# Layer 2's rows go to fixed expert regions of a bucket, right behind the last gather

## The chip, the core and the metric

One core of a Trainium2 chip runs the kernel. The metric is the device time of one execution in microseconds (us), so smaller is better. The engines are PE (TensorE; PEld is its weight load), DVE (VectorE), ACT (ScalarE), POOL (GpSimd) and SP (SyncE, which here only issues DMAs). PE's clock has two levels here, 1.2 and 2.4 GHz; the profile gives the granted clock as a share of full speed (0.5 or 1.0, or a mean of both).

## What is computed

Node features `x` (6250 x 256) pass a two-layer relational graph network over 100000 edges with 8 relations, a linear-attention mixer, and a feed-forward block in which each node uses one of 32 experts:

```python
xn = _layernorm(x)
x = x + gnn(edge_index, edge_type_8, xn) + mix(xn)          # gnn: 2 layers
x = x + ffn(_layernorm(x))

# gnn, each layer l
W = einsum('rb,bio->rio', coeffs[l], bases[l]); h = einsum('ni,rio->rno', x, W)
msg = h[edge_type, src] * deg_inv[dst][:, None]
x_new = segment_sum(msg, dst) + x @ self_loops[l]           # relu after layer 1

# ffn: E = 32 experts, hidden 64
idx = argmax(xf @ router_w.T + router_b)
h = relu(xf . W1[idx] + b1[idx]);  out = relu(h . W2[idx] + b2[idx])
```

## The kernel before

The nodes are cut into NB = 49 blocks of 128. `startup` (L128) norms x, builds the relation weights and writes table 0 (one row per node and relation) to DRAM. `gnn_first` (L541) and `gnn_second` (L812) are the two layers; `experts` (L1063) is the feed-forward block. Each of these is a block of five engine programs with a barrier of all engines at its end.

**A layer.** POOL gathers message rows: each indirect DMA (L487) brings 128 table rows, four DMAs are a group, and the ring holds RG = 16 groups. POOL waits for PE before it uses a group again (L483 to L485). PE sums a block's groups with one-hot matrices that DVE makes (L514, L530), in a loop with run-time bounds. SP counts landed groups. A block's matmul sum opens with a zero matmul (L523) and closes with one (L537). In `gnn_second` each step n also runs stages of other blocks: query, attention, output, norm, router, choice of the expert, and with a lag of 6 blocks the row's rank among the rows of its expert (PE L990 and L991, DVE L905 and L919, in `r.rank`). So the last sum is at step 48 and the last rank at step 54; steps 49 to 54 have no sum.

During `gnn_first`, SP writes zero rows with an out-of-range node number over the whole `bucket` in DRAM (L594, 16 DMAs of 650 KB): rows that no node fills are skipped in the end.

**The experts.** After the barrier, SP loads the weights w1 and w2 (L1107, L1108; 2064 and 2080 KB). They lie where the ring lay. PE counts the rows of each expert (L1158), and DVE turns counts into the tile each expert starts at (L1216 to L1222), each node's row in the bucket (`posi`, L1225 to L1229, blocks 0 to 7 first), and the expert of each tile (`tei`, L1230 to L1234, which ends with `tiles_ok`). POOL scatters the 49 blocks of rows, 260 numbers each, to the bucket (L1125). Experts lie behind each other there, each padded to whole tiles; there are MAXT = 80 tiles at most and all 80 are always processed. When all scatters have landed SP loads the tiles, four to a DMA, into a ring of XS = 40 (L1115). PE runs WARM = 116 matmuls whose result nobody uses (L1164) once `tiles_ok`, the weights and `nearly` (the fifth-last scatter's issue) are there. Then come the 40 pairs of tiles: DVE norms (L1201), PE transposes (L1140), ACT copies (L1254) and copies the pair's weights (L1252), PE multiplies (L1147), ACT adds the bias (L1261), PE multiplies (L1153), DVE adds to the row (L1208), and POOL scatters each tile to `out` (L1131). A tile's ring place is free when that scatter has landed.

## Time and profile before

| | us |
|---|---|
| median of 3 runs | 3634.85 |
| the three runs | 3616.99, 3634.85, 3636.49 |
| the profiled execution | 3627.62 |
| its span, first to last instruction | 3625.9 |

| stretch of the profiled execution, us from the span's start | what runs |
|---|---|
| to 406 | startup |
| 406 to 2010 | gnn_first |
| 2010 to 3366 | gnn_second; the last gather is issued at 3297.7 |
| 3366 to 3461 | experts: tables, scatters, weights, 116 matmuls of no use |
| 3461 to 3619 | experts: 40 pairs of tiles |

Over the span PE is busy 66%, PEld 48%, POOL 45%, DVE 25%, ACT 18%. These are averages over stages with different limits. A table row "start, duration" in the timeline merges neighbouring instructions of one kind (xN), and what stands in brackets is the idle time ahead of it and what ended it.

### The profile page before, as it was taken

What the parts mean: (1) busy time and instruction counts of PE and PEld (TensorE: products, weight loads), DVE (VectorE), ACT (ScalarE), POOL (GpSimd) and SP (SyncE); (2) the same over time, 40 slices, a digit from 0 to 9 for tenths busy, and PEclk for the clock granted to TensorE, in tenths of its full rate; (3) what the DMA queues carried; (4) which work ended last, traced back from release to release, by engine and by line L of the source; (5) the groups of instructions that cost most, each with busy time, mean ns of one, the idle gap of its engine ahead of it and who ended that gap; (6) DMA issues with size and microseconds to landing.
All of it is one profiled execution on the core that took longest, in us unless ns stands there. A gap on an engine that the chain in (4) does not pass through costs nothing. (4 is left out here: it accounts for less than half of the span.)

```text
span 3625.9 us, 37652 instructions
## 1 busy us (share of the span) xinstructions
PE 2399.8 (66%) x9592; PEld 1739.3 (48%) x9592; DVE 915.7 (25%) x2885; ACT 652.3 (18%) x1423; POOL 1649.7 (45%) x1712
## 2 busy tenths in 40 slices
PE   6999346666666666666578356676666667657287
PEld 3777234444444444444456244454444545445065
DVE  2210112222222222222123023233332323324233
ACT  4555101110111011111111101111212112110033
POOL 0000654445444444445451646556565555652535
PEclk9999668878887888778789678777777777878577
DMA  8655533333333333333332323333333333321341
GB/s 220 231 218 195 156 95 112 106 107 103 112 102 104 103 110 109 106 103 113 100 121 75 121 77 92 89 88 91 87 90 88 89 92 89 90 84 46 128 128 53
DMA packets 155518, 401.32 MB, mean 111 GB/s; under 512 B 35102, under 2 KB 86657, under 8 KB 140348
## 3 DMA queue, kind: packets, MB, share of 16 engines
q0 software_dynamic: 81648, 219.65, 20.8%
q10 hardware_dynamic: 36156, 126.22, 9.0%
q1 hardware_dynamic: 37585, 53.92, 5.5%
q8 instruction: 58, 0.95, 0.1%
q14 instruction: 71, 0.58, 0.1%
HBM read 262.69 MB, written 141.04 MB: 111 GB/s over the span
## 5 line engine op out<-in xcount | busy, mean ns | idle before, releaser
L487 POOL DMA_INDIRECT gnn_ring<-table,g_idx x1564 | 1513.1, 967 | 1627.0 <-PE gnn_pagg L530 857.3
L530 PE MATMUL gnn_pagg<-gnn_ring,gnn_oh 128*128 x3904 | 1124.5, 432 | 427.7 <-issue 378.6
L530 PEld LDWEIGHTS gnn_pagg<-gnn_ring,gnn_oh 128*128 128x128 f32 x3904 | 775.7, 212 | 775.3 <-issue 662.9
L514 DVE TENSOR_TENSOR gnn_oh<-gnn_col,g_dst 128x256 f32<-128x256 f32 x976 | 408.3, 426 | 1803.6 <-DVEq L49 1609.9
L715 PE MATMUL gnn_pm<-gnn_whigh,gnn_high 128*128 128x512 f32 x392 | 202.4, 516 | 480.1 <-ACT gnn_rows L769 473.1
L769 ACT COPY gnn_rows<-gnn_pm 128x512 f32<-128x512 f32 x196 | 110.9, 587 | 1320.9 <-DMA pre_bs<-in_L_gnn_bases 1082.7
L715 PEld LDWEIGHTS gnn_pm<-gnn_whigh,gnn_high 128*128 128x128 f32 x392 | 94.4, 241 | 520.0 <-ACT gnn_rows L769 493.4
L1026 ACT ACTIVATE gnn_qe<-gnn_pq,gnn_bq 128x128 f32<-128x128 f32 x98 | 36.0, 368 | 1061.1 <-remote 1045.6
L715 PE MATMUL gnn_pm<-gnn_wlow,gnn_high 128*128 128x512 f32 x392 | 188.0, 480 | 0.0
L715 PE MATMUL gnn_pm<-gnn_whigh,gnn_low 128*128 128x512 f32 x392 | 186.7, 476 | 0.0
L366 PE MATMUL pre_psum<-pre_whigh,pre_high 128*128 128x512 f32 x392 | 157.5, 402 | 10.6 <-DVE pre_low L294 8.1
L366 PE MATMUL pre_psum<-pre_whigh,pre_low 128*128 128x512 f32 x392 | 153.7, 392 | 0.0
L366 PE MATMUL pre_psum<-pre_wlow,pre_high 128*128 128x512 f32 x392 | 153.3, 391 | 0.0
L417 ACT COPY pre_rows<-pre_psum 128x512 f32<-128x512 f32 x196 | 114.6, 589 | 118.1 <-PE pre_psum L366 108.4
L1131 POOL DMA_INDIRECT out<-g_xT x80 | 80.0, 1000 | 99.9 <-DVE g_xT L1208 78.8
L715 PEld LDWEIGHTS gnn_pm<-gnn_whigh,gnn_low 128*128 128x128 f32 x392 | 94.9, 242 | 25.0
L715 PEld LDWEIGHTS gnn_pm<-gnn_wlow,gnn_high 128*128 128x128 f32 x392 | 96.4, 246 | 18.7
L696 PE MATMUL gnn_pk<-gnn_wkv,g_xT 128*128 128x512 f32 x196 | 98.0, 623 | 0.0
L1125 POOL DMA_INDIRECT bucket<-rt_x,exp_posi x49 | 51.2, 1045 | 89.4 <-DVE exp_posi L1229 74.7
L366 PEld LDWEIGHTS pre_psum<-pre_whigh,pre_high 128*128 128x128 f32 x392 | 74.1, 189 | 25.1 <-DVE pre_low L294 8.5
L366 PEld LDWEIGHTS pre_psum<-pre_whigh,pre_low 128*128 128x128 f32 x392 | 73.9, 188 | 15.9
L366 PEld LDWEIGHTS pre_psum<-pre_wlow,pre_high 128*128 128x128 f32 x392 | 74.2, 189 | 14.2
(172 smaller groups left out, 2210.0 us busy)
## 6 DMA issues: line engine op xcount, KB each, us to landing
table<-pre_rows ACTq DMA_DIRECT2D x49, 1024.0 KB
table<-gnn_rows ACTq DMA_DIRECT2D x48, 1024.0 KB
gnn_ring<-table,g_idx POOLq DMA_INDIRECT x1564
pre_bs<-in_L_gnn_bases SPq DMA_DIRECT2D x64, 240.0 KB
bucket<-gnn_zrow SPq DMA_DIRECT2D x16, 650.0 KB
g_xT<-bucket SPq DMA_DIRECT2D x20, 520.0 KB, 6.3
x1T<-gnn_x1T ACTq DMA_DIRECT2D x49, 128.0 KB
gnn_x1T<-x1T ACTq DMA_DIRECT2D x49, 128.0 KB, 2.1
```

The lines of the kernel that those rows point to most:

```text
L366: mm = nc.tensor.matmul(psum[:, n, 0:hi - lo], x[i][:, h, :], w[j][:, h, lo:hi], start=(h == i + j == 0), stop=(h == H2 - 1 and i == 1))
L417: nc.scalar.copy(rows[:, b % 2, lo:hi], psum[:, n, 0:hi - lo]).then_inc(chunk_free, 1)
L487: eng.indirect_dma_start(self.ring[:, q % RG, t, 0:D], None, self.g.table[self.l][:, :], bass.IndirectOffsetOnAxis(ap=self.g.idx[:, at:at ...
L514: self.nc.vector.tensor_tensor(self.oh[:, h, :, :], self.col[:, :].unsqueeze(1).to_broadcast([P, n, P]), self.g.dst[:, ds(q * TPG + h * n, ...
L530: mm = nc.tensor.matmul(pagg[:, k, 0:self.width], self.oh[:, h, i, :], self.ring[:, ds(q & (RG - 1), 1), t, 0:self.width].rearrange("p o n ...
L696: mm = nc.tensor.matmul(pk[:, :], g.xT[:, h, b * P:(b + 1) * P], wkv[:, h, :], start=(h == 0), stop=(h == H2 - 1))
L715: mm = nc.tensor.matmul(pm[:, n % W, 0:CW], x[i][:, h, :], w[j][:, h, n * CW:(n + 1) * CW], start=(h == i + j == 0), stop=(h == H2 - 1 and ...
L769: ins = nc.scalar.copy(rows[:, k, n * CW:(n + 1) * CW], pm[:, n % W, 0:CW])
L1026: nc.scalar.activation(qe[:, k, h, :], pq[:, h * P:(h + 1) * P], ACT.Exp, bias=bq[:, h:h + 1])
L1125: eng.indirect_dma_start(g.bucket[:, :], bass.IndirectOffsetOnAxis(ap=posi[:, b:b + 1], axis=0), r.x2[:, b, :], None).then_inc(scattered, 16)
L1131: eng.indirect_dma_start(out[:, :], bass.IndirectOffsetOnAxis(ap=xb[:, t % XS, D:D + 1].bitcast(I32), axis=0), xb[:, t % XS, 0:D], None, b ...
```

## The change

- The bucket has 6400 rows for each expert (CAP) and 128 spare ones. A row's place is expert x 6400 + rank, which needs no counts. PE adds expert x 6400 to the rank with one more matmul in each of 49 steps (new L1009), and DVE turns the sum into an integer with one more instruction in each (new L943). `g.placed` counts blocks whose places are known.
- POOL's 49 scatters stand behind its last gather in `gnn_second`. The first waits for 38 placed blocks, each one after block 37 for its own.
- `gnn_second` and `experts` are one block of programs: no barrier and no clearing of semaphores between them. The experts' work on SP, PE, ACT and DVE waits for `g.left` = 2 instead (DVE and ACT done with `gnn_second`).
- A tile's first row comes from a table (`rowi`). An expert's last tile is its last 128 rows, so it can share rows with the tile ahead of it; `skip` marks these, and DVE puts the mark into the node number with one more instruction per tile (new L1223). Only the first 128 rows of each expert and the spare ones are written with zeros ahead: 8 DMAs of 4 x 128 rows and one of 128, instead of 16 of 5 x 128.
- DVE's work for the positions goes; instead of one multiply-sized and one reduce instruction over 2560 elements there are three and three.
- SP loads one tile per DMA, from an address in a register, into a ring of XS = 20; it waits for `tiles_ok` as well as for the scatters.

```diff
-XS, XG = 40, 4
+XS, XG = 20, 4
+CAP = 6400
...
-        self.bucket = dram("bucket", (MAXT * P, ROW), F32)
+        self.bucket = dram("bucket", (E * CAP + P, ROW), F32)
...
             def zeros(q):
 
-                if q % 12 == 6 and q // 12 < ZERO:
-                    c = q // 12
-                    eng.dma_start(g.bucket[c * ZT * P:(c + 1) * ZT * P, :].rearrange("(t p) d -> p t d", p=P),
-                                  zrow[:, :].unsqueeze(1).to_broadcast([P, ZT, ROW])).then_inc(zeroed, 16)
+                c, at = divmod(q, 20)
+                if at == 6 and c < FILLS:
+                    first = g.bucket[0:E * CAP, :].rearrange("(e c) d -> c e d", c=CAP)[0:P, c * EF:(c + 1) * EF, :]
+                    eng.dma_start(first, zrow[:, :].unsqueeze(1).to_broadcast([P, EF, ROW])).then_inc(zeroed, 16)
+                elif at == 6 and c == FILLS:
+                    eng.dma_start(g.bucket[E * CAP:, :], zrow[:, :]).then_inc(zeroed, 16)
...
+            for b in range(NB):
+                if b == 0 or b > SURE:
+                    eng.wait_ge(g.placed, max(b, SURE) + 1)
+                eng.indirect_dma_start(g.bucket[:, :], bass.IndirectOffsetOnAxis(ap=r.posi[:, b:b + 1], axis=0),
+                                       r.x2[:, b, :], None).then_inc(g.scattered, 16)
+                if b == NB - 5:
+                    eng.sem_inc(g.nearly, 1)
...
+                if ranked:
+                    V.tensor_copy(r.posi[:, ds(n - 6, 1)], r.rank[:, ds(n - 6, 1)]).then_inc(g.placed, 1)
...
+            eng.wait_ge(g.placed, NB)
+            eng.sem_inc(g.left, 1)
...
-                    nc.tensor.matmul(po[:, k, D:D + E], g.one[:, :], r.acc[:, j, :], start=True, stop=False)
+                    nc.tensor.matmul(po[:, k, D:D + E], g.one[0:2, :], ecap[:, :], start=True, stop=False)
+                    nc.tensor.matmul(po[:, k, D:D + E], g.one[:, :], r.acc[:, j, :], start=False, stop=False)
...
+            nc.scalar.copy(idle[:, 1:2], bq[:, 0:1]).then_inc(g.left, 1)
...
-        x_in = [s.sem(f"x_in{k}") for k in range(XS // XG)]
+        x_in = [s.sem(f"x_in{k}") for k in range(XS)]
-        block = ctx.enter_context(nc.Block())
...
+            eng.wait_ge(g.left, 2)
             eng.dma_start(w1[:, :, :], a["ffn_first"]).then_inc(w_in, 16)
             eng.dma_start(w2[:, :, :], a["ffn_second"]).then_inc(w_in, 16)
+            eng.wait_ge(tiles_ok, 1)
             eng.wait_ge(scattered, 16 * NB)
-            for c in range(MAXT // XG):
-                lo = c * XG % XS
-                for u in range(lo, lo + XG):
-                    if c * XG >= XS:
-                        eng.wait_ge(landed[u], 16 * (c * XG // XS))
-                eng.dma_start(xb[:, lo:lo + XG, :], g.bucket[c * XG * P:(c + 1) * XG * P, :].rearrange("(t p) d -> p t d", p=P)
-                              ).then_inc(x_in[c % (XS // XG)], 16)
+            for t in range(MAXT):
+                if t % XG == 0:
+                    at = values(rowi[0:1, t:t + XG], engines=[eng.engine], min_val=0, max_val=E * CAP,
+                                skip_runtime_bounds_check_because="a tile lies in its expert's rows or the spare ones")[1]
+                if t >= XS:
+                    eng.wait_ge(landed[t % XS], 16 * (t // XS))
+                eng.dma_start(xb[:, t % XS, :], g.bucket[ds(at[t % XG], P), :]).then_inc(x_in[t % XS], 16)
...
-            for b in range(NB):
-                if b == 0 or b == EARLY:
-                    eng.wait_ge(pos_ok, 1 if b == 0 else 2)
-                eng.indirect_dma_start(g.bucket[:, :], bass.IndirectOffsetOnAxis(ap=posi[:, b:b + 1], axis=0),
-                                       r.x2[:, b, :], None).then_inc(scattered, 16)
-                if b == NB - 5:
-                    eng.sem_inc(nearly, 1)
...
-            eng.wait_ge(nearly, 1)
+            eng.wait_ge(g.nearly, 1)
...
-                if t % XG == 0:
-                    eng.wait_ge(x_in[t % XS // XG], 16 * (t // XS + 1))
+                eng.wait_ge(x_in[t % XS], 16 * (t // XS + 1))
...
                 x = xb[:, t % XS, :]
+                node = x[:, D:D + 1].bitcast(I32)
+                V.tensor_tensor(node, node, skip[:, t:t + 1], ALU.max)
                 V.tensor_scalar(xf[:, t % 8, :], x[:, 0:D], x[:, D + 1:D + 2], x[:, D + 2:D + 3],
                                 ALU.subtract, ALU.mult).then_inc(xf_ok, 1)
...
+            V.memset(last[:, E:], float(E * CAP))
+            seq(V.tensor_scalar(over[:, :], cnt[:, 0, :], -float(2 * P - 1), 0.0, ALU.add, ALU.max))
+            seq(V.scalar_tensor_tensor(out=last[:, 0:E], in0=g.iota[:, 0:E], scalar=float(CAP), in1=over[:, :],
+                                       op0=ALU.mult, op1=ALU.add))
+            V.tensor_tensor(step[:, 1, :], last[:, 1:], last[:, 0:E], ALU.subtract)
...
-            seq(V.tensor_scalar(cnt[:, 3, :], cnt[:, 2, :], float(P), None, ALU.mult))
...
-            for lo, hi in ((0, EARLY), (EARLY, NB)):
-                seq(V.tensor_tensor(by_block(part, lo, hi), by_block(r.oh, lo, hi),
-                                    cnt[:, 3, :].unsqueeze(1).to_broadcast([P, hi - lo, E]), ALU.mult))
-                seq(V.tensor_reduce(pos[:, 0, lo:hi], by_block(part, lo, hi), AX.X, ALU.add))
-                seq(V.tensor_tensor(pos[:, 1, lo:hi], pos[:, 0, lo:hi], r.rank[:, lo:hi], ALU.add))
-                V.tensor_copy(posi[:, lo:hi], pos[:, 1, lo:hi]).then_inc(pos_ok, 1)
             seq(V.tensor_tensor(cnt[:, 0, :], cnt[:, 1, :], cnt[:, 2, :], ALU.add))
-            seq(V.tensor_tensor(tl[:, :, :], cnt[0:1, 0, :].unsqueeze(1).to_broadcast([1, MAXT, E]),
-                                g.iota[0:1, 0:MAXT].unsqueeze(2).to_broadcast([1, MAXT, E]), ALU.is_le))
-            seq(V.tensor_reduce(te[:, :], tl[:, :, :], AX.X, ALU.add))
-            V.tensor_scalar(tei[:, :], te[:, :], float(E - 1), None, ALU.min).then_inc(tiles_ok, 1)
+            V.tensor_scalar(step[:, 0, :], cnt[:, 1, :], -float(P), float(CAP), ALU.mult, ALU.add)
+            seq(V.tensor_tensor(tl[:, 0, :, :], cnt[:, 0, :].unsqueeze(1).to_broadcast([P, MAXT, E]),
+                                g.iota[:, 0:MAXT].unsqueeze(2).to_broadcast([P, MAXT, E]), ALU.is_le))
+            for k in range(2):
+                ins = V.tensor_tensor(tl[:, 1 + k, :, :], tl[:, 0, :, :], step[:, k, :].unsqueeze(1).to_broadcast([P, MAXT, E]),
+                                      ALU.mult)
+            seq(ins)
+            for k in range(3):
+                ins = V.tensor_reduce(te[:, k, :], tl[:, k, :, :], AX.X, ALU.add)
+            seq(ins)
+            V.tensor_scalar(tei[:, :], te[0:1, 0, :], float(E - 1), None, ALU.min)
+            seq(V.scalar_tensor_tensor(out=te[:, 3, :], in0=g.iota[:, 0:MAXT], scalar=float(P), in1=te[:, 1, :],
+                                       op0=ALU.mult, op1=ALU.add))
+            seq(V.scalar_tensor_tensor(out=te[:, 1, :], in0=te[:, 2, :], scalar=last[:, 0:1], in1=te[:, 3, :],
+                                       op0=ALU.add, op1=ALU.min))
+            V.tensor_copy(rowi[:, :], te[0:1, 1, :]).then_inc(tiles_ok, 1)
+            V.tensor_copy(part[:, :], g.nodei[:, 0:1])
+            seq(V.tensor_tensor(twice[:, :], te[:, 3, :], te[:, 1, :], ALU.subtract))
+            seq(V.tensor_scalar(skip[:, :], twice[:, :], part[:, 0:1], float(SKIP), ALU.is_gt, ALU.mult))
             for t in range(6):
...
-        gnn_second(nc, g, a, r)
-        nc.clear_and_free_semaphores(nc.allocated_since(had))
-        nc.all_engine_barrier()
-        experts(nc, g, a, r, out)
+        with nc.Block() as block:
+            gnn_second(nc, g, a, r, block)
+            experts(nc, g, a, r, out, block)
```

POOL, from its last gathers to the tiles' scatters. Before (`rt_x` holds the rows, `exp_posi` the places; the semaphore names after "waits" are older ones of the same numbers, here the places of blocks 0 to 7 and of the rest):

```order
L487 DMA gnn_ring<-table,g_idx 128x256 [waits gnn1_pairs]
L487 DMA gnn_ring<-table,g_idx 128x256 x5
L819 UNCONDITIONAL_BRANCH
L1287 ISA [waits barrier_Pool_Activation_PE_DVE_SP_gather]
L1120 UNCONDITIONAL_BRANCH [waits barrier_Pool_Activation_PE_DVE_SP_gather]
L1125 DMA bucket<-rt_x,exp_posi 10240x260 [waits pre_x_in1]
L1125 DMA bucket<-rt_x,exp_posi 10240x260 x7
L1125 DMA bucket<-rt_x,exp_posi 10240x260 [waits pre_x_in1]
L1125 DMA bucket<-rt_x,exp_posi 10240x260 x40
L1131 DMA out<-g_xT 6250x256 [waits pre_var_ok] x80
```

The same place in the change:

```order
L489 DMA gnn_ring<-table,g_idx 128x256 [waits gnn1_pairs]
L489 DMA gnn_ring<-table,g_idx 128x256 x5
L886 DMA bucket<-rt_x,rt_posi 204928x260 [waits g_placed]
L886 DMA bucket<-rt_x,rt_posi 204928x260 x37
L886 DMA bucket<-rt_x,rt_posi 204928x260 [waits g_placed] x11
L1148 UNCONDITIONAL_BRANCH
L1152 DMA out<-g_xT 6250x256 [waits exp_y_ok] x80
```

The 49 scatters have moved ahead of the end of `gnn_second`, and the barrier between them and the gathers is gone.

DVE, from the tiles' first numbers (`exp_cnt`) to `tiles_ok`. Before:

```order
L1225 TENSOR_TENSOR exp_part<-rt_oh,exp_cnt 128x256 [waits g_dve_own]
L1227 TENSOR_REDUCE exp_pos<-exp_part 128x8 [waits g_dve_own]
L1228 TENSOR_TENSOR exp_pos<-exp_pos,rt_rank 128x8 [waits g_dve_own]
L1229 CAST exp_posi<-exp_pos 128x8 [waits g_dve_own]
L1225 TENSOR_TENSOR exp_part<-rt_oh,exp_cnt 128x1312
L1227 TENSOR_REDUCE exp_pos<-exp_part 128x41 [waits g_dve_own]
L1228 TENSOR_TENSOR exp_pos<-exp_pos,rt_rank 128x41 [waits g_dve_own]
L1229 CAST exp_posi<-exp_pos 128x41 [waits g_dve_own]
L1230 TENSOR_TENSOR exp_cnt<-exp_cnt 128x32
L1231 TENSOR_TENSOR exp_tl<-exp_cnt,g_iota 1x2560 [waits g_dve_own]
L1233 TENSOR_REDUCE exp_te<-exp_tl 1x80 [waits g_dve_own]
L1234 TENSOR_SCALAR exp_tei<-exp_te 1x80 [waits g_dve_own]
```

In the change (`g_xT` stands for the table of 3 x 2560 that lies in its memory):

```order
L1251 TENSOR_TENSOR exp_cnt<-exp_cnt 128x32 [waits g_dve_own]
L1252 TENSOR_SCALAR exp_step<-exp_cnt 128x32 [waits g_dve_own]
L1253 TENSOR_TENSOR g_xT<-exp_cnt,g_iota 128x2560
L1256 TENSOR_TENSOR g_xT<-g_xT,exp_step 128x2560 [waits g_dve_own]
L1256 TENSOR_TENSOR g_xT<-g_xT,exp_step 128x2560
L1260 TENSOR_REDUCE exp_te<-g_xT 128x80 [waits g_dve_own]
L1260 TENSOR_REDUCE exp_te<-g_xT 128x80 x2
L1262 TENSOR_SCALAR exp_tei<-exp_te 1x80 [waits g_dve_own]
L1263 SCALAR_TENSOR_TENSOR exp_te<-g_iota,exp_te 128x80
L1265 SCALAR_TENSOR_TENSOR exp_te<-exp_te,exp_last 128x80 [waits g_dve_own]
L1267 CAST exp_rowi<-exp_te 1x80 [waits g_dve_own]
```

The eight instructions on positions are gone; two instructions over 2560 elements have become six, and three small ones follow.

## Rows read from the trace of the kernel before

**Rows 1.** The page: PE's busy tenths in 40 equal slices of the span.

```profile
PE   6999346666666666666578356676666667657287
```

**Rows 2.** Timeline, POOL: last gather, first scatter; start, duration, in brackets idle ahead.

```profile
3297.66 0.95 POOL L487 DMA_INDIRECT gnn_ring<-table,g_idx  x1 [0.30 <-issue]
3373.36 2.02 POOL L1125 DMA_INDIRECT bucket<-rt_x,exp_posi  x1 [74.74 <-DVE exp_posi L1229]
```

**Rows 3.** Source view of the scatters' line: ns min/median/max, first and last start.

```profile
L1125 POOL DMA_INDIRECT bucket<-rt_x,exp_posi x49: 970/974/3399, 3373.4 to 3438.2; - x49
```

**Rows 4.** Timeline, DVE: last rank, then the tables.

```profile
3364.61 0.19 DVE L919 TENSOR_REDUCE rt_rank<-gnn_ch 128x1 f32<-128x32 f32 x1
3366.41 0.48 DVE L1212 MEMSET exp_hT<- 1x512 f32 x1 [1.61 <-PEq L1288]
...
3371.57 0.18 DVE L1222 TENSOR_SCALAR exp_cnt<-exp_cnt 128x32 f32<-128x32 f32 x1
...
3372.98 1.52 DVE L1225 TENSOR_TENSOR exp_part<-rt_oh,exp_cnt 128x1312 f32<-128x1312 bf16 x1
...
3376.42 0.23 DVE L1230 TENSOR_TENSOR exp_cnt<-exp_cnt 128x32 f32<-128x32 f32 x1
3376.70 2.81 DVE L1231 TENSOR_TENSOR exp_tl<-exp_cnt,g_iota 1x2560 f32<-1x2560 f32 x1
...
3382.39 0.19 DVE L1234 TENSOR_SCALAR exp_tei<-exp_te 1x80 int32<-1x80 f32 x1
```

**Rows 5.** Timeline, ACT: its first use of the weights.

```profile
3386.83 0.50 ACT L1252 COPY exp_ws<-exp_w 128x129 f32 x2 [24.59 <-DMA exp_w<-in_ffn_second]
```

**Rows 6.** Timeline, PE: the 116 matmuls and the first transposes.

```profile
3418.92 12.60 PE L1164 MATMUL exp_psum<-rt_oh,g_one 128*128 128x512 bf16 x45 [52.46 <-issue]
...
3444.87 16.11 PE L1164 MATMUL exp_psum<-rt_oh,g_one 128*128 128x512 bf16 x66 [0.82 <-issue]
3460.82 1.04 PE L1140 MATMUL exp_psum<-g_ident,exp_xf 128*128 128x128 f32 x8
```

**Rows 7.** Timeline, SP and DVE: the tiles' loads and the first norms.

```profile
3440.78 33.12 SPq L1115 DMA_DIRECT2D g_xT<-bucket  x11
3444.47 2.87 DVE L1201 TENSOR_SCALAR exp_xf<-g_xT 128x256 f32<-128x256 f32 x8 [61.88 <-DMA g_xT<-bucket]
```

**Rows 8.** Timeline, PE: zero matmuls opening blocks 0, three others, 46, 47 and 48.

```profile
2067.85 0.21 PE L523 MATMUL gnn_pagg<-g_zero 128*128 128x2 bf16 x1
...
2582.10 0.17 PE L523 MATMUL gnn_pagg<-g_zero 128*128 128x2 bf16 x1
2614.85 0.16 PE L523 MATMUL gnn_pagg<-g_zero 128*128 128x2 bf16 x1 [2.41 <-issue]
2634.54 0.17 PE L523 MATMUL gnn_pagg<-g_zero 128*128 128x2 bf16 x1
...
3303.23 0.17 PE L523 MATMUL gnn_pagg<-g_zero 128*128 128x2 bf16 x1
3320.03 0.17 PE L523 MATMUL gnn_pagg<-g_zero 128*128 128x2 bf16 x1
3336.65 0.17 PE L523 MATMUL gnn_pagg<-g_zero 128*128 128x2 bf16 x1
```

**Rows 9.** Timeline, DVE in the pairs of tiles: two pauses.

```profile
3475.76 0.76 DVE L1208 SCALAR_TENSOR_TENSOR g_xT<-exp_psum,g_xT 128x256 f32<-128x256 f32 x2 [3.29 <-DMA gnn_ring<-table,g_idx]
...
3500.08 0.76 DVE L1208 SCALAR_TENSOR_TENSOR g_xT<-exp_psum,g_xT 128x256 f32<-128x256 f32 x2 [3.25 <-DMA gnn_ring<-table,g_idx]
```

**Rows 10.** Source views, us to landing: tiles' scatters (L1131), tiles' loads (L1115).

```profile
DMA to landing us min/median/max: 2.5/2.5/2.5
...
DMA to landing us min/median/max: 3.7/6.3/10.3
```

**Rows 11.** Timeline, PE: the transposes of two pairs in a row, at full clock.

```profile
3465.68 0.60 PE L1140 MATMUL exp_psum<-g_ident,exp_xf 128*128 128x128 f32 x4
...
3468.20 0.60 PE L1140 MATMUL exp_psum<-g_ident,exp_xf 128*128 128x128 f32 x4
```

50 lines of the change are left out of this document (31 added, 19 removed).

## The prediction

> **What bounds the kernel now.** The page's 40 slices come first [rows 1]: in the slices of layer 2 PE is 5 to 7 tenths busy and no engine is full. Then comes one slice, the 38th (3354 to 3445 us), with PE at 2 tenths. That slice is the place of the change. The timeline shows what stands in it. POOL issues its last gather at 3297.66 and its first scatter at 3373.36, 74.74 us later [rows 2]; PE meanwhile drains the ring. The last rank is made at 3364.61, the barrier takes 1.61 us of DVE, and the tables follow [rows 4]. The 49 scatters run from 3373.4 to 3438.2 and set the pace: 64.8 us for 48 steps, 1.35 us each [rows 3]. The first tile load is issued at 3440.78 and the first norm starts at 3444.47 [rows 7]. But PE starts its first transpose only at 3460.82, since the 116 matmuls of no use are still running [rows 6]. So the wait that ends last ahead of the pairs is that of PE for its own 116 matmuls, 16.4 us later than the first tile. From the last rank's end (3364.8) to PE's first transpose it is 96.0 us.
>
> **What goes.** The scatters leave this stretch. At POOL's last gather 38 places have to be known for the first scatter. PE opens block 46 at 3303.23 [rows 8], so step 45 is at its end at 3298, and with a lag of 6 blocks about 40 places are known: the first wait is met at once or within a few us. From 3299, at 0.97 + 0.30 us each, block 40 goes out at about 3351 [rows 2, 3]; the last 8 wait for their ranks, the last of which is made at 3364.8. The last scatter lands about 4 us later. The positions' instructions go as well, and so do the barrier and its 1.6 us.
>
> **What bounds the stretch afterwards.** The tables: PE's 116 matmuls and SP's loads both wait for `tiles_ok`. Before, DVE needed 3366.41 to 3382.58 for them, 16.2 us [rows 4]. Of this 3371.57 to 3376.42 goes, 4.85 us. Two instructions over 2560 elements become six; they cost 2.81 us on one partition. I take the same on 128 partitions, because the one over 1312 elements on 128 partitions takes 1.52 us, 1.16 ns per element beside 1.10 here [rows 4]. That adds 4 x 2.81 = 11.2. Some nine small ones at 0.2 add 1.8. So 16.2 - 4.9 + 11.2 + 1.8 = 24.3 us. The weights were there at 3386.83, 20.4 us after DVE's start on the tables and beside scatters [rows 5]; they stay covered by the tables, by 4 us. The scatters are covered by 20 us.
>
> Then come the 116 matmuls, now alone: the first 13 or so at PE's lower clock of 1.2 GHz at 0.43 us, the others at 0.215. The two runs of 45 and 66 show this: 12.6 and 16.1 us, the second with 8 at the lower clock [rows 6]. That is 5.6 + 22.1 = 27.7 us. The tile loads hide behind them: the first norm came 3.7 us after the first load [rows 7], 20 loads of 133 KB are fewer bytes than the 40 tiles before.
>
> Handover from layer 2: 0.5 us. Sum: 0.5 + 24.3 + 27.7 = 52.5 us in place of 96.0. **Gain 43.5 us**, if layer 2 ends when it did.
>
> **What it costs ahead of that.** (a) POOL now sends scatters while PE, DVE and ACT drain the ring. Before, that stretch had no DMAs of POOL, and blocks 46 and 47 took 16.8 and 16.6 us; under gathers 46 blocks took 1235.4 us, 26.9 each [rows 8]. Part of the 26.9 is POOL's own pace (16 gathers at 0.95 + 0.30 us are 20 us [rows 2]), which scatters don't impose. The rest looks like starved engines. The same is seen where PE's 116 matmuls run beside scatters: from 3431.5 to 3444.87 PE starts only 116 - 45 - 66 = 5, where it does one in 0.215 to 0.43 us otherwise [rows 6]. Bounds: nothing, and two blocks (what fits into the 52 us of scatters without a pause) at 26.9 instead of 16.7, 20 us. A small gain from a shift of the steps can't be excluded, but no row shows one. I take 15, nearer to the upper end, since the row of the 116 matmuls is of scatters themselves.
>
> (b) One matmul and one copy more in each of 49 steps. A small DVE instruction lasts 0.2 us [rows 4], and its successor can overlap part of it; PE's lasts no longer. Nothing if they fall into a pause of their engine, 0.2 us per step if they are on the path in full: 0 to 10 us. I take 5, the middle.
>
> (c) In the pairs: DVE has two more small instructions per pair (0.2 us each at most), beside 0.76 for the results and 2 x 0.36 for the norms [rows 7, 9] in a pair of 2.52 us at the full clock [rows 11]. Its slack is 1.0 us, so nothing; at most 0.4 x 40 = 16 us if it had none. SP issues 80 loads instead of 20 and reads four addresses for four of them; eleven issues took 33 us only because they waited for places [rows 7]; it has 1.25 us per tile. Nothing.
>
> (d) The ring of 20. A tile's place goes round: scatter 1.0 us, landing 2.5, SP's turn 0.5, load 3.7 (up to 10.3 with four tiles in one DMA) [rows 3, 10]: 8 us, 14 at worst. Between the result of tile t and the norm of tile t+20 DVE works on seven pairs, 17.6 us at the full clock. Nothing.
>
> (e) Seven fewer fill DMAs in layer 1, 6 MB of writes in some 1500 us: nothing.
>
> **Sum.** 43.5 - 15 - 5 = 23.5 us off 3627.6, the profiled execution's own time: 3604. This execution lies 7.2 us below the median of the three runs and 10.6 above the lowest. I put the forecast a little above, at **3608**, between the profile's sum and the median's (3611).
>
> The Trainium skill ("Runtime: NRT & Kernel Launch", section on instruction fetch mechanics) says that instructions come in blocks of 256 and that crossing from one to the next is mostly hidden. By that rule nothing starves beside POOL's DMAs and term (a) would be zero. The trace speaks against it in the pairs: there DVE stands still for 3.29 and 3.25 us at 3475.76 and 3500.08, 24 us apart [rows 9], about as long as 256 of PE's instructions last.
>
> **Rivals.**
> 1. The drain is not disturbed: (a) is 0 and (b) small. Scatters move as many bytes as gathers, but it was only one slow piece in 65 us of them [rows 3, 6]. Then 43.5 - 2.5 = 41 us: 3587 on the profile, about 3592. Chance 0.22. The rule of the skill above leads here.
> 2. The 116 matmuls meet another slow piece and the drain costs its full 20, the steps 10: 43.5 - 20 - 10 - 12 = 1.5 us gained, 3626 to 3634. For it: the slow piece took 13.4 us once [rows 6]. Against: POOL is silent then. Chance 0.12.
> 3. The ring of 20 starves the pairs: if the round trip were 25 us instead of 8, each of three turns of the ring would wait some 7 to 10 us, 25 us in all: about 3630. Against: the sum in (d). Chance 0.08.
> 4. Slower: the added instructions shift layer 2's pauses. Its blocks come in two kinds, as 32.8 and 19.7 us in a row [rows 8]; each that turns from short to long costs about 13 us. With two more long ones the gain of 23.5 is gone; with four the kernel is about 29 us slower, near 3660. For it: 26.9 is a mean of both kinds, so the mix matters. Against: the change adds 98 PE instructions to a layer with thousands. Chance 0.08.
>
> That the scatters start no earlier (the first wait not met) would show as a POOL pause after 3298; a few us of it cost nothing, since block 48's rank ends the row.
>
> **How the numbers follow.** Forecast (3596 to 3620) 0.50; rivals 0.22, 0.12, 0.08, 0.08. The range takes in rival 1, the forecast, and rivals 2 and 3: 3586 to 3634; below it lies little, above it rival 4. A measurement tells 0.5% (18 us) from no change here. Faster by over 0.5% means under 3616.7: rival 1 and nearly all of the forecast, 0.67. Within 0.5%: the rest of the forecast and rivals 2 and 3, 0.23. Slower: rival 4 and a little of the others, 0.10.
>
> **What would show it.** First scatter within 5 us of the last gather, the last landed before the tables end. Blocks 46 and 47 between 17 and 27 us long: their length decides between the forecast and rival 1. `tiles_ok` 24 to 25 us after the last place; PE's 116 matmuls in 28 us; first transpose 52 to 53 us after layer 2's end. From PE's first transpose to the end about 165 us as before; waits of the norms for their loads would be rival 3. Blocks 1 to 46 of layer 2 at 26.9 us plus 0.1: more is rival 4. The prediction is wrong if DVE's instructions over 2560 elements cost more on 128 partitions, or if something outside this stretch moves.

## The result, and the profile after

The changed kernel takes 3643.09 us (median of 15 runs, 3634.79 to 3650.49), the kernel before, measured beside it, 3629.56 us (15 runs, 3612.07 to 3645.48). The ratio is 1.0048 with a 95% interval of 1.0031 to 1.0065: a little slower, where 3608 us and a gain were forecast. The profiled execution of the changed kernel took 3639.18 us, with a span of 3637.4 us and a mean granted clock of 0.807 (before: 3627.62, 3625.9 and 0.801).

The head of the experts' part came out as forecast. Behind the last rank stand the tables and then PE's 116 matmuls, without a slow piece. The rows are DVE's and PE's timeline of the changed kernel (start, duration, in brackets the idle time before and what ended it), to be read beside [rows 4] and [rows 6]:

```profile
3428.51 0.15 DVE L943 CAST rt_posi<-rt_rank 128x1 int32<-128x1 f32 x1
...
3452.64 0.19 DVE L1267 CAST exp_rowi<-exp_te 1x80 int32<-1x80 f32 x1
```

```profile
3452.89 26.97 PE L1186 MATMUL exp_psum<-rt_oh,g_one 128*128 128x512 bf16 x116 [23.86 <-DVE exp_rowi L1267]
3479.69 1.04 PE L1161 MATMUL exp_psum<-g_ident,exp_xf 128*128 128x128 f32 x8
```

From the last rank's end (3428.7) to the end of `exp_rowi` it is 24.2 us, where 0.5 + 24.3 were forecast; the 116 matmuls take 27.0 (27.7). PE's first transpose starts 51.0 us behind the last rank, in place of 96.0.

What was gained there was lost one stage earlier. The scatters do start right behind the last gather, and 40 of them go out without a pause, as POOL's timeline shows (line 489 gathers, line 886 scatters):

```profile
3309.62 0.95 POOL L489 DMA_INDIRECT gnn_ring<-table,g_idx  x1 [0.30 <-issue]
3310.87 1.00 POOL L886 DMA_INDIRECT bucket<-rt_x,rt_posi  x1 [0.30 <-issue]
...
3360.67 0.97 POOL L886 DMA_INDIRECT bucket<-rt_x,rt_posi  x1 [0.30 <-issue]
3382.19 0.97 POOL L886 DMA_INDIRECT bucket<-rt_x,rt_posi  x1 [20.55 <-DVE rt_posi L943]
```

Meanwhile block 46 of layer 2 stands. PE's timeline has the zero matmuls (line 525) that open blocks 46, 47 and 48, to be read beside the last of [rows 8], and the sums over the ring between them, and ahead of them the matmuls (line 1020) whose result ACT takes next; then come the one row of DVE and the one of ACT that end their idle time:

```profile
3314.14 0.53 PE L1020 MATMUL gnn_pq<-gnn_rw,gnn_turned 128*128 128x32 f32 x4
3315.04 0.17 PE L525 MATMUL gnn_pagg<-g_zero 128*128 128x2 bf16 x1
3316.97 2.18 PE L532 MATMUL gnn_pagg<-gnn_ring,gnn_oh 128*128 x8 [1.76 <-PEq L50]
3368.89 12.80 PE L532 MATMUL gnn_pagg<-gnn_ring,gnn_oh 128*128 x40 [49.74 <-PEq L50]
3384.47 0.17 PE L525 MATMUL gnn_pagg<-g_zero 128*128 128x2 bf16 x1
3386.57 10.54 PE L532 MATMUL gnn_pagg<-gnn_ring,gnn_oh 128*128 x40 [1.93 <-issue]
3399.90 0.17 PE L525 MATMUL gnn_pagg<-g_zero 128*128 128x2 bf16 x1
```

```profile
3368.12 0.76 DVE L516 TENSOR_TENSOR gnn_oh<-gnn_col,g_dst 128x256 f32<-128x256 f32 x2 [51.59 <-DVEq L50]
```

```profile
3365.68 0.18 ACT L1049 COPY gnn_lg<-gnn_pq 128x32 f32<-128x32 f32 x1 [64.70 <-remote]
```

Block 46 takes 3384.47 - 3315.04 = 69.4 us in place of 16.8; block 47 takes 15.4. PE did one turn of its loop over groups and DVE one of its, and then nothing ran but POOL. The three don't stand in the same way. Line 50 belongs to the helper `take`, which waits for a semaphore. PE waits there for DVE's next one-hots: the first is made at 3368.54, and PE goes on at 3368.89. DVE waits for a free place for its one-hots, which PE's 8 matmuls had given it by 3319.15, yet it goes on only at 3368.12. ACT has what it waits for at 3314.67 and goes on 51.0 us later. So what has to be explained is why DVE and ACT stand; PE, here, waits for DVE. The table by stretch (busy time and number of instructions of each engine) says it in one line:

```profile
core 0: us, PE busy (x) PEld busy (x) DVE busy (x) ACT busy (x) POOL busy (x), PEclk, DMA share, GB/s
...
3330.00:3362.00 32.00, 0.00 (x0) 0.00 (x0) 0.00 (x0) 0.00 (x0) 24.26 (x25) 0.50 0.29 104
3368.00:3384.00 16.00, 14.94 (x55) 11.09 (x56) 7.76 (x30) 0.00 (x0) 0.97 (x1) 0.80 0.02 7
```

In 32 us three engines execute no instruction, while the DMA engines are 29% busy. ACT goes on 4.0 us and DVE 6.5 us after the issue of POOL's 40th scatter ends at 3361.6. No transfer or result that these two wait for ends there: POOL merely pauses.

The balance, changed kernel less kernel before, in the two profiled executions: layer 1 and all ahead +5.1 us (layer 2 opens at 2072.9 in place of 2067.85; 4.6 of it stand already at the opening of layer 1's first block, 410.3 in place of 405.7); blocks 0 to 45 of layer 2 +6.7 (1242.1, 1235.4); from the opening of block 46 to the last rank 113.6 in place of 61.6, +52.0; head of the experts' part -45.0; pairs to the last scatter of rows -7.3. The sum is +11.5, and the spans differ by 11.5.

### The profile page after: what moved, and what is told of

It reads as the page before. It is cut to its first block and busy times, and to the rows that moved or that the text cites. A ratio compares the mean times of both kernels' runs of the same rounds, so it can differ in the third digit from the quotient of the medians.

```text
span 3637.4 us, 38090 instructions
## 1 busy us (share of the span) xinstructions
PE 2394.4 (66%) x9641; PEld 1733.6 (48%) x9641; DVE 931.1 (26%) x3022; ACT 651.4 (18%) x1424; POOL 1643.4 (45%) x1712
## 5 line engine op out<-in xcount | busy, mean ns | idle before, releaser
L489 POOL DMA_INDIRECT gnn_ring<-table,g_idx x1564 | 1510.3, 966 | 1640.8 <-PE gnn_pagg L532 868.2
L368 PE MATMUL pre_psum<-pre_wlow,pre_high 128*128 128x512 f32 x392 | 154.6, 394 | 0.0
L1030 PE MATMUL gnn_pnd<-g_kvn,gnn_qf 128*128 128x132 f32 x196 | 42.4, 299 | 81.9 <-issue 76.9
```

The lines of the kernel that those rows point to most:

```text
L368: mm = nc.tensor.matmul(psum[:, n, 0:hi - lo], x[i][:, h, :], w[j][:, h, lo:hi], start=(h == i + j == 0), stop=(h == H2 - 1 and i == 1))
L489: eng.indirect_dma_start(self.ring[:, q % RG, t, 0:D], None, self.g.table[self.l][:, :], bass.IndirectOffsetOnAxis(ap=self.g.idx[:, at:at ...
L1030: mm = nc.tensor.matmul(pnd[:, k, h * (P + C):(h + 1) * (P + C)], qf[:, j, h, :], g.kvn[:, h, :], start=True, stop=True)
```

## The experiments

Everything turned on what stops DVE and ACT, and through DVE also PE, for 50 us. Theory A: GpSimd's stretch of DMAs without a pause. Theory B: the traffic of these DMAs. Theory C: a busy GpSimd, whatever it does. Theory D: the merged drain itself, with its added instructions. One fact must be known first. The runs fell on two kinds of chips. On one the kernel before takes 3626 to 3664 us, as in the result above; on the other 2611 to 2614, and there nobody stands still. Below they are called the 3630 kind and the 2610 kind. No chip is on record at two different times, so whether the kind belongs to the chip or to a state that it was in is not shown. Each ratio is to the kernel before on the same chip.

**The scatters behind the drain again.** Everything else of the change stays:

```diff
             for b in range(NB):
-                if b == 0 or b > SURE:
-                    eng.wait_ge(g.placed, max(b, SURE) + 1)
+                if b == 0:
+                    eng.wait_ge(g.placed, NB)
```

> Undo one part: the scatters wait for the last block's rank, as in the kernel before, and all else of the change stays. Theory A (while GpSimd issues its scatters without a pause, TensorE, VectorE and ScalarE stand still, and this made block 46 of layer 2 take 69.4 us in place of 16.8): block 46 takes about 17 us again, from its opening to the last rank about 62 us (113 in the changed kernel); the scatters then stand behind the last rank, 45 of them are issued some 48 us after it and the 116 warm matmuls (27.7 us) follow, so the first transposes come some 75 us behind the last rank (52.4 in the changed kernel): 51 less and 23 more, about 3615 us, ratio to the kernel before about 0.996. Theory D (the merged blocks of the drain and their added instructions are slow by themselves): block 46 still takes about 69 us and the time is the changed kernel's plus 23, about 3665 us, ratio 1.010.

It fell on the 2610 kind: 2611.41 us, ratio 1.0001 (0.9992 to 1.0010). It tells nothing on the theories, but much on the kernel. These are the first rows of the list of waits of this run, behind the same row of the changed kernel on the 3630 kind (us in total, times, longest):

```profile
DVE gnn_oh L516 <- DVEq L50: 1620.3, 633, 51.6
```

```profile
DVE gnn_oh L516 <- DVEq L50: 1006.9, 886, 6.2
ACT gnn_rows L773 <- PE gnn_pm L719: 745.0, 195, 20.1
```

DVE waits no longer than 6.2 us at its one-hot loop. POOL issues all 782 gathers of a layer in one row, one each 1.25 us, without ever waiting for PE; a block of layer 2 takes 20.0 us on average, and GpSimd alone sets the pace. The same kernel again, on the other kind:

> The kernel with the scatters behind the last rank, on another chip than the first time (there no engine stood still beside gathers or scatters). Where the kernel before takes some 3630 to 3670 us, theory A: block 46 takes about 17 us in place of 69.6, the first transposes come some 75 us behind the last rank, the time is about 28 us under the changed kernel's, ratio to the kernel before 0.996 to 0.999. Theory D: block 46 stays at about 69 us, ratio 1.010 or more.

3622.71 us, ratio 1.0000 (0.9981 to 1.0019). Block 46 takes 17.0 us in place of 69.4. Theory D falls: merged as it is, the drain runs at its old pace without scatters beside it. The last rank stands at 3374.3, 64.7 us behind the last gather. The head took longer than expected, 89.9 us in place of 75. PE's timeline of this run says why:

```profile
3422.32 12.79 PE L1186 MATMUL exp_psum<-rt_oh,g_one 128*128 128x512 bf16 x45 [47.48 <-POOLq L889]
3435.29 0.38 PE L1186 MATMUL exp_psum<-rt_oh,g_one 128*128 128x512 bf16 x1 [0.18 <-issue]
3438.09 0.38 PE L1186 MATMUL exp_psum<-rt_oh,g_one 128*128 128x512 bf16 x1 [2.42 <-issue]
...
3447.90 16.49 PE L1186 MATMUL exp_psum<-rt_oh,g_one 128*128 128x512 bf16 x66 [1.53 <-issue]
```

```profile
3441.55 0.97 POOL L886 DMA_INDIRECT bucket<-rt_x,rt_posi  x1 [0.30 <-issue]
```

The 116 matmuls took 42 us, not 27.7. After the first 45, PE runs one matmul each 2.1 to 2.8 us; it goes on at full pace 5.4 us after GpSimd is done (3442.5). These matmuls wait for nothing; the slow piece of [rows 6] was the same thing.

**The changed kernel with pauses in the scatters.**

```diff
+                if b and b % 8 == 0:
+                    eng.wait_ge(g.scattered, 16 * b)
                 eng.indirect_dma_start(g.bucket[:, :], ...
```

> The changed kernel, but before each eighth scatter GpSimd waits until all its scatters so far have landed, which makes six pauses of 2 to 4 us. Theory A in its strong form (the others go on as soon as GpSimd pauses): block 46 is cut to some 25 to 40 us, and the time falls by 25 to 45 us under the changed kernel's, to about 3600 to 3615. Theory A in its weak form (the others need a pause of 4 us or more, the time that they took to resume in the changed kernel): the pauses are too short, block 46 takes 69 us plus the pauses, up to 85, and the time rises by up to 10 us over the changed kernel's. Theory B (the traffic of the scatters slows the others, whoever issues them): the same bytes in somewhat more time, block 46 within 10 us of 69.

On the 2610 kind: 2613.97 us, ratio 1.0005 (0.9996 to 1.0014). On the 3630 kind:

> The changed kernel with a wait for all its landed scatters before each eighth, on another chip. Strong theory A (the others go on as soon as GpSimd pauses): block 46 takes 25 to 45 us, ratio about 0.993. Weak theory A (they need a longer pause than a landing's 2 to 4 us): block 46 takes 69 to 85 us, ratio 1.005 to 1.008. Theory B (traffic): within 10 us of 69, ratio 1.003 to 1.008.

3609.52 us, ratio **0.9961** (0.9946 to 0.9976): the change now gains. POOL's timeline shows a pause, and PE's the openings of blocks 46 and 47:

```profile
3322.50 0.97 POOL L888 DMA_INDIRECT bucket<-rt_x,rt_posi  x1 [0.30 <-issue]
3325.60 0.97 POOL L888 DMA_INDIRECT bucket<-rt_x,rt_posi  x1 [2.13 <-DMA bucket<-rt_x,rt_posi]
```

```profile
3317.64 0.17 PE L525 MATMUL gnn_pagg<-g_zero 128*128 128x2 bf16 x1
...
3350.09 0.17 PE L525 MATMUL gnn_pagg<-g_zero 128*128 128x2 bf16 x1
```

Block 46 takes 32.5 us. The same scatters carry the same bytes; only pauses of 1.9 to 2.8 us were added, and 37 us went. The length of the block is what theory A's strong form forecast, and it leaves no room for B in its plain form, which wanted 59 to 79 us. But the others did not go on as soon as GpSimd paused:

```profile
3329.25 0.18 ACT L1051 COPY gnn_lg<-gnn_pq 128x32 f32<-128x32 f32 x1 [25.70 <-issue]
3333.06 0.42 DVE L516 TENSOR_TENSOR gnn_oh<-gnn_col,g_dst 128x256 f32<-128x256 f32 x1 [13.93 <-DVEq L50]
```

That is 5.8 and 9.6 us after the last issue ahead of the pause had ended (3323.47), while the next eight scatters were already on their way; and from there DVE made the block's other one-hots beside scatters, waiting 1.75 us at most. A pause frees the engines for longer than it lasts. Each pause waits for all landings, so the runs don't part GpSimd's issuing from its transfers still on their way. From the last gather to PE's first transpose it is 138.7 us here (ratio 0.9961), 154.6 with the late scatters (1.0000), 163.2 in the kernel before and 170.1 in the changed kernel (1.0048). The ratios stand in that order, except that late scatters and the kernel before can't be told apart.

**The changed kernel once more**, to see both kinds of chip in one argument:

> The changed kernel itself once more, next to the kernel before, since the four runs so far fell on a chip on which the kernel before takes 2612.78 us in place of 3629.56 and the other engines don't stand still beside GpSimd's gathers (VectorE's longest wait at its one-hot loop is 6.2 us there and 51.6 us in the profiled run of the changed kernel). Theory A (the freeze of the drain beside the scatters made the change slower): where the other engines stand still beside the gathers, in a kernel of some 3630 us, block 46 takes about 69 us again and the ratio is about 1.005; where they don't, in a kernel of some 2610 us, block 46 takes 15 to 20 us and the changed kernel is faster, by what its head stretch gains (about 30 to 45 us), ratio 0.983 to 0.989. Theory D (the merged drain is slow by itself): the change doesn't gain on either chip, ratio 1.000 or above.

It fell on the 3630 kind: 3686.74 us beside 3664.49, ratio 1.0058 (1.0045 to 1.0071). Block 46 took 69.6 us (3359.78 to 3429.38). The changed kernel itself wasn't run on the 2610 kind.

**Pauses in the gathers.** If an unbroken stretch is harmful, the layers themselves must suffer, since POOL sends its gathers there mostly 16 in a row (one row has 24, and the first of a layer 72 or 64). The trace of the kernel before has it too: POOL's, ACT's and DVE's timelines in its blocks 43 and 44 (line 487 gathers).

```profile
3238.84 0.95 POOL L487 DMA_INDIRECT gnn_ring<-table,g_idx  x1 [4.62 <-PE gnn_pagg L530]
...
3257.86 0.94 POOL L487 DMA_INDIRECT gnn_ring<-table,g_idx  x1 [0.30 <-issue]
```

```profile
3261.69 0.37 ACT L1026 ACTIVATE gnn_qe<-gnn_pq,gnn_bq 128x128 f32<-128x128 f32 x1 [21.39 <-remote]
```

```profile
3262.84 0.42 DVE L514 TENSOR_TENSOR gnn_oh<-gnn_col,g_dst 128x256 f32<-128x256 f32 x1 [7.82 <-DVEq L49]
```

Both go on 3 to 4 us after the 16th gather. DVE did not stand through all of it: it made one-hots until 3245.3 and two more at 3251.05 and 3254.60. The edit makes GpSimd wait for its own transfers before each fourth group of four gathers:

```diff
+            if q and q % 4 == 0:
+                eng.wait_ge(self.landed[(q - 1) % RG], 16 * sum(...))
             for t in range(min(TPG, NT - q * TPG)):
```

> The changed kernel with a pause in the gathers too: in both layers GpSimd waits, before each fourth group, until the group before has landed, so it never issues more than 16 gathers without a pause of some 2 us (98 waits in all). If a pause of 2 us lets the other engines go on, the blocks of the gather phase (26.9 us each on average in layer 2, 98 in both layers) shorten wherever GpSimd had issued over 16 in a row: a gain of 0 to 100 us. If it doesn't, the pauses add what GpSimd has no slack for: it is busy 940 of the 1242 us of layer 2, so 0 to 60 us slower. Block 46 and the scatters stay as in the changed kernel.

3320.01 us, ratio **0.9181** (0.9134 to 0.9227). The list of waits has 72 waits for its own gathers, 155.6 us in all; with them the kernel is 306 us shorter than the kernel before on that chip, three times the most that was expected. Block 46, whose scatters have no pause here, still takes 69.2 us. Pauses before each second group, with batched scatters, should give more; the next three runs of this kernel all fell on the 2610 kind:

> The changed kernel with both pauses: gathers wait for the landing of the group before ahead of each second group (so at most 8 go without a pause), scatters ahead of each eighth. If it is the uninterrupted stretch that stops the others (16 gathers in a row still stood still for up to 20 us with pauses at each fourth group), shorter stretches give more: 3320 less 0 to 150 us, and block 46 takes about 32 us as with batched scatters in place of 69, so 37 us less again: 3130 to 3290 us. GpSimd's own bound is 782 gathers by 1.25 us plus 98 pauses of about 2 us, 1174 us a layer. If the gain of the pauses came from something else than the length of the stretches, the added 98 pauses cost and the time is above 3320. On a chip where nobody stands still (kernel before 2613 us) the pauses can only cost, up to 400 us.

> Pauses after each eighth gather and each eighth scatter, on another chip than before (there, where no engine stood still, they cost 357 us, 2971 in place of 2614). Where the kernel before takes 3630 to 3670 us, theory A (the length of GpSimd's stretch without a pause is what counts): 3130 to 3290 us, block 46 about 32 us. If the pauses' gain comes from elsewhere: above 3320.

2970.93 us, ratio 1.1360 (1.1341 to 1.1379), and 2970.39 us, 1.1369 (1.1350 to 1.1388): there pauses only cost, 357 us for two layers, and a block of layer 2 takes 23.6 us on average in place of 20.0, which is GpSimd's own pace with its pauses. A kernel with the same pauses in the gathers, with late scatters and with the added work of the next part's two diffs (SyncE's transfers behind GpSimd's) did fall on the 3630 kind:

> One kernel with several places to read. Gathers: a pause ahead of each second group in both layers, so at most 8 in a row. Layer 1's drain: GpSimd clears a small tile 160 times behind its last gather (59 us, added work). Layer 2's drain: scatters late; GpSimd issues 38 plain transfers behind its last gather (20 us), and when they have landed SyncE issues 38 (20 us; both added work). Where engines stand still beside the gathers (kernel before 3630 to 3670 us): if a busy GpSimd is enough, the first block behind layer 1's last gather takes 60 us or more, else about 20; if GpSimd's plain transfers do it, VectorE's one-hots stop for 15 us or more during them and block 46 takes 35 us or more; if any transfers do it, the one-hots stop beside SyncE's too; if only indirect ones, no block of the drain takes over 20 us. The blocks of layer 2 that gather take 24 to 25 us on average in place of 26.9 if shorter stretches help (98 waits of 2 us are then GpSimd's own bound of 24), layer 1 about 1200 to 1300 us in place of 1663. Where none stands still, it tells only what the pauses cost.

3080.75 us beside 3635.21, ratio **0.8467** (0.8443 to 0.8492). The stretches of both layers with gathers, by the table of stretches: layer 1 and layer 2 of the changed kernel, then with a pause per 16 gathers, then per 8, and last the late scatters' run on the 2610 kind, without pauses.

```profile
412.00:2072.00 1660.00, 1046.05 (x3955) 757.82 (x3954) 346.54 (x945) 197.06 (x461) 781.34 (x809) 0.80 0.32 102
2073.00:3315.00 1242.00, 797.70 (x3304) 585.05 (x3303) 392.34 (x1420) 191.84 (x391) 711.16 (x741) 0.78 0.30 88
```

```profile
412.00:1782.00 1370.00, 1044.43 (x3955) 747.72 (x3954) 346.73 (x945) 199.13 (x460) 761.49 (x788) 0.85 0.38 122
1783.00:2976.00 1193.00, 799.99 (x3294) 582.85 (x3295) 392.77 (x1420) 192.04 (x391) 733.70 (x761) 0.79 0.33 94
```

```profile
412.00:1600.00 1188.00, 984.79 (x3803) 716.07 (x3803) 333.72 (x909) 189.57 (x424) 752.53 (x812) 0.92 0.42 135
1611.00:2755.00 1144.00, 789.90 (x3406) 607.91 (x3405) 393.91 (x1444) 202.47 (x423) 740.41 (x828) 0.86 0.34 99
```

```profile
412.00:1400.00 988.00, 920.21 (x3905) 680.93 (x3903) 344.08 (x932) 196.32 (x441) 731.21 (x764) 0.99 0.52 165
1425.00:2370.00 945.00, 745.84 (x3374) 571.90 (x3373) 401.04 (x1452) 192.90 (x394) 718.45 (x744) 0.90 0.41 117
```

The windows don't hold quite the same work, as the numbers of instructions show: for layer 1 the first two reach to the opening of layer 2, the third ends where the last block opens and the fourth a little behind that block; for layer 2 the third begins 64 us early. By the zero matmuls, from the opening of layer 1's first block to that of its last it is 1579.3, 1315.5, 1192.4 and 965.7 us, and from that of layer 2's block 0 to that of block 46 1242.1, 1194.1, 1079.7 and 920.5: most of the gain is layer 1's. DVE and ACT are busy for about the same time everywhere, PE for less only as its clock rises; what changes is the idle time around them. With a pause per 8 gathers a block of layer 2 takes 23.5 us on the 3630 kind and 23.6 on the other (1079.7 and 1087.8 us for blocks 0 to 45): GpSimd is the bound, and hardly anything is left of the standing still. The granted clock (the third figure from the end) rises as PE's idle time shrinks, from 0.80 to 0.92 in layer 1, and gives a part of the time back.

**What about GpSimd's stretch it is.** Late scatters, and in their old place added work: SyncE's plain transfers of the same rows, or GpSimd's, or a GpSimd that clears a small tile and moves nothing. The two diffs show GpSimd's plain transfers and the clearing; the late scatters are left out.

```diff
             agg.gather(eng)
+            eng.wait_ge(g.placed, 38)
+            for b in range(38):
+                eng.dma_start(g.extra[b * P:(b + 1) * P, :], r.x2[:, b, :]).then_inc(g.extra_ok, 16)
```

```diff
             agg.gather(eng)
+            for b in range(160):
+                eng.memset(busy[:, :], 0.0).then_inc(busied, 1)
+                eng.wait_ge(busied, b + 1)
```

> The scatters late as in the run before, and in their old place, right behind the last landing of the gathers, SyncE issues 38 plain transfers of the same rows and bytes to memory that nothing reads (added work). Theory A (GpSimd's issuing is what stops the others): block 46 takes about 17 us, as with late scatters alone. Theory B (the writes themselves are what stops the others): block 46 takes clearly longer than 17 us, 40 or more.

> As the run before, but GpSimd issues the 38 plain transfers, right behind its last gather. Theory A: TensorE, VectorE and ScalarE stand still for as long as these issues last (38 of 0.6 to 1.0 us, 23 to 38 us), block 46 takes about 40 to 55 us. If only indirect transfers of GpSimd stop the others, or the traffic alone does and SyncE's transfers have shown nothing: about 17 us.

> Scatters late, and SyncE issues 38 plain transfers of the rows in their old place (added work), on a chip where the others do stand still. Theory A (GpSimd's issue of indirect transfers stops the others): block 46 takes about 17 us, as with late scatters alone. Theory B (the writes themselves): 40 us or more.

> As the run before, but GpSimd issues the 38 plain transfers right behind its last gather. If any transfer that GpSimd issues stops the others: block 46 takes 40 to 55 us. If only indirect ones do: about 17 us.

> Scatters late, and GpSimd clears a small tile 160 times in their old place (added work, no transfers), some 0.3 us each and about 55 us in all. Theory C (a busy GpSimd stops the others, by a shared port or otherwise): block 46 takes 40 us or more. Theory A in the form that transfers are needed for it: about 17 us.

> Scatters late, SyncE's 38 plain transfers in their old place (added work). GpSimd's own issuing as the cause: block 46 takes about 17 us. The writes themselves: 40 us or more. Where no engine stands still (kernel before about 2613 us) it tells nothing.

> Scatters late; added work in both drains: GpSimd issues 38 plain transfers behind its last gather of layer 2, and clears a small tile 160 times (some 59 us) behind its last gather of layer 1, where blocks take about 20 us. If any transfer of GpSimd stops the others: block 46 of layer 2 takes 35 to 55 us; if only indirect ones: about 17. If a busy GpSimd stops them: the first block behind layer 1's last gather takes 60 us or more; if not: about 20.

All seven fell on the 2610 kind and decide nothing: 2613.84, 2614.40, 2618.26, 2614.09, 2647.22, 2614.32 and 2656.80 us. The two with the cleared tile are longer; in layer 2 the gathers end there only 24 us before the last rank, so 59 us of clearing don't fit beside the drain; in the last run the clearing lies behind layer 1, and layer 2 opens 43 us later. The kernel mix2 asked again, at several places, and it fell on the 3630 kind. In its layer 1 drain GpSimd clears tiles for 59 us; DVE, in its one-hot loop, goes on beside it:

```profile
1583.39 59.01 POOL L624 MEMSET gnn_busy<- 128x256 f32 x160
```

```profile
1600.99 0.42 DVE L521 TENSOR_TENSOR gnn_oh<-gnn_col,g_dst 128x256 f32<-128x256 f32 x1 [5.32 <-DVEq L50]
1601.86 0.42 DVE L521 TENSOR_TENSOR gnn_oh<-gnn_col,g_dst 128x256 f32<-128x256 f32 x1 [0.44 <-DVEq L50]
```

The block that opens at 1578.98 takes 20.6 us: theory C falls for a GpSimd that clears. One that reads and computes was not tried. GpSimd's 38 plain transfers came late, since the paused gathers ran until 2815, so they lie beside block 48 alone:

```profile
2815.26 20.23 POOL L899 DMA_DIRECT2D extra<-rt_x  x38
```

```profile
2814.97 6.68 PE L537 MATMUL gnn_pagg<-gnn_ring,gnn_oh 128*128 x16 [3.20 <-PEq L50]
```

```profile
2830.41 0.43 DVE L946 TENSOR_TENSOR gnn_xb<-gnn_xb,gnn_bo 128x256 f32<-128x256 f32 x1 [5.10 <-DMA gnn_xb<-in_x]
```

PE runs sums beside them and DVE is held up once, for 5.1 us, by a transfer that is late; from the opening of block 48 to the last rank it took 33.0 us, 28.0 in the kernel before. So plain transfers of GpSimd don't bring the standstill in this place, but only the last turns of the loops fall into it. SyncE's transfers came behind the last rank, where no loop runs, and decide nothing.

**Is the change worth anything with pauses?**

```diff
 (the kernel before)
+            if q and q % 2 == 0:
+                eng.wait_ge(self.landed[(q - 1) % RG], 16 * sum(...))
```

> The changed kernel with pauses after each eighth gather and each eighth scatter. If it falls on a chip where engines stand still beside the gathers (kernel before 3610 to 3670 us): 3030 to 3080 us, that is the 3081 us of the kernel with added work in the drains, less what its late scatters and added transfers cost. On one where none stands still: 2970 us again.

> The kernel before, with nothing but the pause of the gathers ahead of each second group. Theory (the change pays only as far as the drain behind the last gather is long, and pauses make the gathers the bound, so that it is some 25 us long): the time is 0 to 20 us above gp2b8_d's, ratio of the two 0.993 to 1.000. Rival (the change's head stretch is worth its 43 us once nothing stands still): 35 to 50 us above it. Against the kernel without pauses: about 15% faster where engines stand still, about 13% slower where they don't.

Both fell on the 2610 kind: 2968.37 us (1.1362) and 2980.84 us (1.1417, 1.1398 to 1.1436). The ratio of the two medians is 0.9958, 12.5 us, inside what was expected if the drain's length sets the worth of the change. The source view of these two kernels gives it (first and last start). In the changed one the last scatter starts 60 us behind the last rank's cast, and PE's transposes start at 2851.4; in the other the scatters end at 2852.6 and the transposes start at 2861.0:

```profile
L890 POOL DMA_INDIRECT bucket<-rt_x,rt_posi x49: 965/971/2757, 2751.1 to 2833.9; - x49
L947 DVE CAST rt_posi<-rt_rank x49: 153/154/155, 1752.2 to 2773.9; 128x1 int32<-128x1 f32 x49
L1165 PE MATMUL exp_psum<-g_ident,exp_xf x160: 270/272/328, 2851.4 to 2947.4; 128*128 128x128 f32 x160
```

```profile
L1127 POOL DMA_INDIRECT bucket<-rt_x,exp_posi x49: 967/971/3405, 2787.9 to 2852.6; - x49
L1142 PE MATMUL exp_psum<-g_ident,exp_xf x160: 270/272/329, 2861.0 to 2956.9; 128*128 128x128 f32 x160
```

The last rank stands 24 us behind the last gather (2749.8), not 67, so at most 24 of the 65 us of scatters can be hidden.

## Why the prediction was wrong

*The head, 43.5 us gained:* right. Handover and tables took 24.2 us (24.8), the warm matmuls 27.0 (27.7), the whole 51.0 (52.5).

*Term (a), the drain beside scatters, 15 us with bounds of 0 and 20:* this is the step that failed. It cost 52 us. The upper bound took two blocks at 26.9 us, what a block costs beside gathers. But in the gather phase POOL stops, mostly after 16 transfers, to wait for PE, and in each such stop the others go on; the 40 scatters have no stop. The price of a stretch isn't a rate per block but nearly the stretch itself: 40 x 1.27 = 51 us of scatters, less the 5.7 us that DVE still ran beside them, and 6.5 us until it went on. That is the 51.6 us that DVE stood, and block 46 lost 52.6. The row that says so was among those quoted: in [rows 6] PE starts 5 matmuls in 13.4 us beside scatters. Taken at its word, as a standstill until POOL is done, it gives a bound of some 52 us, the prediction's own length for the scatters without a pause, and a forecast near 3640. It was used as a hint for a value within bounds that came from the wrong stretch.

*Term (b), 5 us for one matmul and one copy per step:* 6.7 us measured over 46 blocks, in one execution of each kernel; right within what they can tell. That some 40 places would be known at the last gather was right too.

*Terms (c), (d) and (e), nothing:* the pairs became 7.3 us shorter (150.9 us from the first transposes to the end of the last scatter of rows, 158.3 before), so the ring of 20 doesn't starve them (rival 3). Layer 1, from its first block to its last, took 1579.3 us in place of 1578.2; what lies ahead of it was 4.6 us longer, for which the code gives no reason.

*The rivals:* rival 1 (3592, drain undisturbed) fell by block 46. Rival 2 had the right direction, "the drain costs its full 20", and the same bound that was too low; its other half, a slow piece in the 116 matmuls, didn't occur, since POOL was silent. Rival 4's shift of pauses among the blocks did not show: blocks 0 to 45 moved by 6.7 us in all.

*On the rule* that rival 1 leaned on: that nothing starves beside POOL's DMAs is contradicted by the trace of the changed kernel, more strongly than by the pauses of [rows 9]. The same section of the Trainium skill ("Runtime: NRT & Kernel Launch", Instruction fetch mechanics) has another sentence, which the prediction passed over: a taken branch to code outside the part that is held forces a fetch before execution can go on. The runs agree with that in part: DVE stopped at the second turn of its loop, and DVE's tables, with no loop in them, ran through beside scatters in mix2. Other rows don't fit it. ACT's program of this layer has no loop, and it stood as well. The straight code of PE's 116 matmuls ran for just 45 and then crawled, in [rows 6] and in the run with late scatters. And the profile lists two DMA queues of the kind "instruction", with 59 and 73 packets in the changed kernel. Neither has a packet between 3288.8 and 3381.5, so none arrives when ACT and DVE go on at 3365.7 and 3368.1; nor has either one between 3425.6 and 3448.9 in the run with late scatters, where PE crawls. So that the engines lacked instructions is possible, but these traces don't show it, and what held DVE and ACT stays open. The view of the DMA queues shows only POOL's own queue between 3330 and 3362 in the changed kernel, at 29%:

```profile
q0 software_dynamic: 1200, 3.33, 29.0%
```

*What stays open:* why DVE and ACT stand still beside GpSimd's indirect DMAs on one kind of chip and not on the other; whether it is the issuing or the transfers on their way; whether SyncE's transfers, or GpSimd's plain ones beside whole loops, would do it; and what the changed kernel itself takes on the 2610 kind, where its variants with late and with batched scatters are even with the kernel before. A version that beats both kernels on both kinds wasn't found: batched scatters gain 0.4% on one and nothing on the other, paused gathers gain up to 15% on one and lose 14% on the other.

## What to carry to other kernels

When work of one engine is moved beside that of others, don't price it by the average of a stretch with the same kind of work: look for the longest piece without a pause, and at whether the others ran at all within it. Where they don't, short waits of the issuing engine for its own transfers can be worth far more than they cost. And a gain that lies in hiding work behind a drain is only as large as the drain, which shrinks as soon as the producer becomes the bound.

## What the runs showed of the hardware

- On one kind of chip DVE and ACT executed nothing for some 50 us, though what they waited for was there, while GpSimd issued 40 indirect DMAs 1.27 us apart, with the DMA engines 29% busy, and they went on 6.5 and 4.0 us after it paused; PE waited for DVE. A pause of 2 us after each 8 cut the block from 69.4 us to 32.5.
- PE, running matmuls that wait for nothing beside such DMAs, did 45 at full pace and then one each 2.1 to 2.8 us until 5.4 us after GpSimd was done.
- Clearing tiles on GpSimd for 59 us without transfers held up nobody (a block of 20.6 us beside it).
- The same kernel took 2611 to 2614 us on four chips and 3626 to 3664 us on others, with the busy time of POOL's gathers equal (1506.4 and 1510.3 us for 1564) and DVE's longest wait in its loop 6.2 us in place of 51.6.
- Pauses after each 8 gathers, in two different kernels, took 15% off the time on the one kind (3080.75 us beside 3635.21) and added 14% on the other (2980.84 beside 2611.41).
